# Two feed-forward stages of a decoder kernel, from loops over chunks to code written out as pipelines

## The reference

```python
def _layernorm(x, axis=-1, eps=1e-05):
    m = jnp.mean(x, axis=axis, keepdims=True)
    v = jnp.var(x, axis=axis, keepdims=True)
    return (x - m) / jnp.sqrt(v + eps)

def _L2_ffn_ref(x, weight, gate_w, lora_U, lora_V):
    scaling = 1.0 / lora_U.shape[1]
    B, S, D_in = x.shape
    xt = x.reshape(-1, D_in)
    gate = jax.nn.softmax(xt @ gate_w.T, axis=-1)
    base = xt @ weight.T
    t = jnp.einsum('nh,erh->ner', xt, lora_U)
    lora = jnp.einsum('ne,eor,ner->no', gate, lora_V, t)
    out = base + scaling * lora
    return out.reshape(B, S, -1)

def _L3_ffn_ref(x, weight):
    b_weight = jnp.sign(weight)
    return jnp.einsum('bsi,oi->bso', x, b_weight)
...
    x = x + _L2_ffn_ref(_layernorm(x, axis=-1), L2_ffn_weight, L2_ffn_gate_w, L2_ffn_lora_U, L2_ffn_lora_V)
...
    x = x + _L3_ffn_ref(_layernorm(x, axis=-1), L3_ffn_weight)
```

## Time and profile before

| | us |
|---|---|
| three runs | 3691.47, 3686.51, 3674.39 |
| median | 3686.51 |
| profiled execution, its time | 3691.43 |
| its span in the profile | 3689.4 |
| TensorE busy | 3116.8 (84%) |
| VectorE busy | 1856.5 (50%) |
| ScalarE busy | 1345.1 (36%) |

### The profile page before, as it was taken

The page is one execution under the profiler, slowest core; times in us unless marked ns, Lnnn a source line. Parts: engine busy times, 40 slices in busy tenths (PEclk is TensorE's granted clock), DMA queues, the critical chain, the costliest instruction groups (busy, mean ns, idle before and its releaser), DMA issues. The chain is left out here.

```text
span 3689.4 us, 47172 instructions
## 1 busy us (share of the span) xinstructions
PE 3116.8 (84%) x17330; PEld 1949.8 (53%) x17330; DVE 1856.5 (50%) x3060; ACT 1345.1 (36%) x2260; POOL 1142.4 (31%) x964
## 2 busy tenths in 40 slices
PE   5769999999999979999986929996867666898786
PEld 3444555545545458788844626764645543343354
DVE  3365666555666653242287521112568456556574
ACT  2223444444444443333243523332324233334452
POOL 0015666665666620000053331112323021011230
PEclk9879999999999989999988959997988776669987
DMA  3010000000000011111000071222010000000000
GB/s 109 0 48 1 1 1 1 1 1 1 1 1 1 1 36 52 52 41 52 14 14 32 1 258 27 34 33 47 2 31 1 6 9 2 1 1 1 10 18 26
DMA packets 110937, 89.27 MB, mean 24 GB/s; under 512 B 20459, under 2 KB 104197, under 8 KB 110725
## 3 DMA queue, kind: packets, MB, share of 16 engines
q1 hardware_dynamic: 101509, 75.73, 6.9%
q0 software_dynamic: 7152, 8.55, 1.3%
q10 hardware_dynamic: 2064, 2.10, 0.2%
HBM read 68.33 MB, written 18.94 MB: 24 GB/s over the span
## 5 line engine op out<-in xcount | busy, mean ns | idle before, releaser
L684 POOL TENSOR_TENSOR acc<-acc,pf 128x512 f32<-128x512 f32 (+1 forms) x448 | 564.1, 1281 | 254.2 <-ACT pf L811 254.0
L868 DVE TENSOR_REDUCE mxa<-ps 128x1 f32<-128x512 f32 x512 | 327.3, 681 | 229.1 <-PE ps L730 227.2
L811 ACT ACTIVATE pf<-ps 128x512 f32<-128x512 f32 x512 | 278.0, 595 | 318.7 <-PE ps L705 293.9
L718 PE MATMUL ps<-pf,v 128*64 128x512 f32 (+1 forms) x1152 | 311.0, 618 | 0.0
L3374 DVE TENSOR_REDUCE mx<-ps 128x2 f32<-128x1024 f32 (+1 forms) x192 | 184.0, 958 | 159.4 <-PE ps L3268 118.4
L3362 ACT ACTIVATE pT<-ps 128x1024 f32<-128x1024 f32 (+1 forms) x192 | 153.2, 811 | 222.3 <-PE ps L3280 221.8
L1678 POOL TENSOR_TENSOR e<-e,sm 128x1232 f32<-128x1232 f32 x48 | 107.9, 2249 | 228.7 <-DVE sm L1933 228.7
L730 PE MATMUL ps<-kH,qH 64*128 64x512 f32 x512 | 158.0, 443 | 23.9 <-DVE mc L876 18.5
L1065 POOL TENSOR_TENSOR x<-x,ys 128x256 f32<-128x256 f32 x16 | 11.9, 742 | 508.3 <-DVE ys L1270 508.3
L3264 PE MATMUL ps<-kT,qT 64*128 64x512 f32 (+2 forms) x384 | 102.1, 529 | 65.5 <-DVE mx L3374 58.9
L1736 PE MATMUL ps<-ident,e 128*77 128x128 f32 x768 | 123.9, 313 | 25.8 <-ACT pT L1843 24.6
(11 more groups left out here) (521 smaller groups left out, 7134.9 us busy)
## 6 DMA issues: line engine op xcount, KB each, us to landing
w_raw<-in_c_h SPq DMA_DIRECT2D x32, 512.0 KB, 3.9
w1a<-in_f_w SPq DMA_DIRECT2D x8, 1024.0 KB
w2a<-in_f_w SPq DMA_DIRECT2D x8, 1024.0 KB
moe_rows<-pad SPq DMA_DIRECT2D x1, 5167.5 KB, 20.1
xs<-moe_rows SPq DMA_DIRECT2D x39, 132.5 KB, 2.1
w_raw<-in_c_w SPq DMA_DIRECT2D x32, 128.0 KB, 2.3
x<-in_x SPq DMA_DIRECT2D x1, 2048.0 KB, 8.2
moe_acc<-x ACTq DMA_DIRECT2D x1, 2048.0 KB
```

The costliest lines, as they stand in the source:

```text
L684: pool.tensor_tensor(now[0:r, :], now[0:r, :], pf[0:r, n % RING, a, :], ALU.add).then_inc(added.sem, 1)
L718: ins = pe.matmul(g.bk(3)[SIDE[a], :], v[0:r, u // 2 % 2, t, u % 2 * P + a * HD:u % 2 * P + (a + 1) * HD], pf[0:r, n % RING, a, :], start= ...
L811: act.activation(pf[0:r, n % RING, a, :], g.bk(bk.bank[f"s{n}_{a}"])[0:r, :], ACT.Exp, bias=bias)\
L868: dve.tensor_reduce(mxa[:, q % 2, half, a, j:j + 1], g.bk(4 + a), AXX, ALU.max).then_inc(bk.release(f"m{q}_{i}_{a}"), 1)
```

## The change

In both stages `ln_block` is gone: its statistics are at the head of the one block that is left, before the chunks. The loops are written out, and the work of neighbouring chunks is interleaved. z and t have two buffers, zT three in the gated ffn and two in the last; ScalarE makes both copies of zT. In the gated ffn gates and parts of four tiles share two banks instead of four, tT has one, and the outputs rotate over three banks; in the last ffn the outputs rotate over six. The gate weights have a semaphore of their own. The output is stored two tiles at a time, 256 KB, as soon as they are added.

```diff
@@ -2762,96 +2762,162 @@
...
+        z, zT = sb("z", [P, 2, TC, D]), sb("zT", [P, 3, KD, CH])
+        t, gate, mx = sb("t", [P, 2, TC, E * R]), sb("gate", [P, TC, E]), sb("mx", [P, TC])
-        bk = Banks(g, [("t0", 0), ("t1", 1), ("p0", 2), ("p1", 3), ("p2", 4), ("p3", 5), ("tT", 6)]
-                   + [(f"y{j}", [7, 0, 1, 2][j]) for j in range(TC)])
...
-        ln_block(g, load_weights)
+        fills = []
+        for c in range(NC):
+            fills += [(f"t0_{c}", 0), (f"t1_{c}", 1), (f"p0_{c}", 2), (f"p1_{c}", 3), (f"tT_{c}", 4)]
+        fills += [(f"y{i}", 5 + i % 3) for i in range(NT)]
+        bk = Banks(g, fills)
...
+        parts = g.ps[:, 2:4, :].rearrange("p b (a n) -> p b a n", a=2)
...
+            @block.sync
+            def _(sp):
+                load(sp, gus[:], rows(gu), gate_in)
+                load(sp, w[:], rows(W), w_in)
+                load(sp, v[:], V, w_in)
...
-                with pe.Fori(0, NC) as c:
-                    pe.wait_ge(*z_made.at(c, 1))
-                    turn(g, pe, bk, c, ("t0", "t1"), z4)
...
+                def turn_tokens(c):
+                    pe.wait_ge(*z_made.at(0, c + 1))
+                    for k in range(KD):
+                        pe.wait_ge(*bk.free(f"t{k}_{c}", 0))
+                        for j in range(TC):
+                            ins = pe.transpose(g.bk(k)[:, j * P:(j + 1) * P], z[:, c % 2, j, k * P:(k + 1) * P], g.ident[:])
+                        ins.then_inc(bk.fill(f"t{k}_{c}"), 1)
+                def gates_and_parts(c):
+                    for k in range(KD):
+                        pe.wait_ge(*bk.read(f"t{k}_{c}", 0))
...
+                            for k in range(KD):
+                                ins = pe.matmul(g.bk(2 + b)[:, a * D:a * D + ER], zT[:, c % 3, k, j * P:(j + 1) * P], gus[:, k, :],
+                                                start=k == 0, stop=k == KD - 1)
+                        ins.then_inc(bk.fill(f"p{b}_{c}"), 1)
+                def output(c):
+                    pe.wait_ge(*t_made.at(0, c + 1))
+                    pe.wait_ge(*bk.free(f"tT_{c}", 0))
...
+                    for j in range(TC):
...
+                        pe.wait_ge(*bk.free(name, 0))
...
+                            pe.matmul(out, zT[:, c % 3, k, tile], w[:, k, :], start=k == 0, stop=False)
+                        pe.wait_ge(*bk.read(f"tT_{c}", 0))
+                        pe.matmul(out, tT[:, tile], v[:], start=False, stop=True).then_inc(bk.fill(name), 1)
+                turn_tokens(0)
+                pe.wait_ge(*gate_in.at(0, 16))
+                for c in range(-1, NC):
+                    if c + 1 < NC:
+                        gates_and_parts(c + 1)
+                    if c + 2 < NC:
+                        turn_tokens(c + 2)
+                    if c == 0:
+                        pe.wait_ge(*w_in.at(0, 32))
+                    if 0 <= c:
+                        output(c)
             @block.scalar
             def _(act):
-                with act.Fori(0, NC) as c:
-                    act.wait_ge(*bk.full("t0", c))
-                    act.activation(zT[:, 0, :], g.bk(0), ACT.Copy).then_inc(bk.release("t0"), 1)
...
+                def tokens(c):
+                    for k in range(KD):
+                        act.wait_ge(*bk.full(f"t{k}_{c}", 0))
+                        if c >= 3:
+                            act.wait_ge(*bk.full(f"y{TC * (c - 2) - 1}", 0))
+                        act.activation(zT[:, c % 3, k, :], g.bk(k), ACT.Copy).then_inc(bk.release(f"t{k}_{c}"), 1)
+                ln_stats_scalar(g, act, NT, spread, rooted)
+                tokens(0)
+                for c in range(-1, NC):
+                    if c + 2 < NC:
+                        tokens(c + 2)
+                    if c + 1 < NC:
+                        act.wait_ge(*logit.at(0, c + 2))
+                        act.activation(gate[:], gate[:], ACT.Exp).then_inc(expd.sem, 1)
+                    if 0 <= c:
+                        act.wait_ge(*bk.full(f"tT_{c}", 0))
+                        if c:
+                            act.wait_ge(*bk.full(f"y{TC * c - 1}", 0))
+                        act.activation(tT[:], g.bk(4), ACT.Copy).then_inc(bk.release(f"tT_{c}"), 1)
             @block.vector
             def _(dve):
-                with dve.Fori(0, NC) as c:
-                    link = Chain(dve, step, c)
-                    normalise(g, dve, c, z4).then_inc(z_made.sem, 1)
-                    dve.wait_ge(*bk.full("t1", c))
-                    dve.tensor_scalar(zT[:, 1, :], g.bk(1), 1.0, None, ALU.mult).then_inc(bk.release("t1"), 1)
...
+                link = Chain(dve, step, 0)
+                def normalised(c):
+                    if c >= 2:
+                        dve.wait_ge(*bk.full(f"t{KD - 1}_{c - 2}", 0))
...
+                        i = TC * c + j
+                        ins = dve.tensor_scalar(z[:, c % 2, j, :], g.x[:, i, :], g.mean[:, i:i + 1], g.rstd[:, i:i + 1], ALU.subtract, ALU.mult)
+                    ins.then_inc(z_made.sem, 1)
+                def gated(c):
+                    quad = lambda a: a.rearrange("p (b a) -> p b a", a=2)
+                    eight = mx[:].unsqueeze(2).broadcast_to([P, TC, E])
+                    for b in range(2):
+                        dve.wait_ge(*bk.full(f"p{b}_{c}", 0))
...
+                    link(dve.tensor_tensor(gate[:], gate[:], eight, ALU.mult))
+                    if c >= 2:
+                        dve.wait_ge(*bk.full(f"tT_{c - 2}", 0))
...
+                        ins.then_inc(bk.release(f"p{b}_{c}"), 1)
+                    for b in range(2):
+                        dve.wait_ge(*bk.read(f"p{b}_{c}", 0))
                     dve.sem_inc(t_made.sem, 1)
+                def added(c):
+                    for i in range(TC * c, TC * (c + 1)):
+                        dve.wait_ge(*bk.full(f"y{i}", 0))
+                        dve.tensor_tensor(g.x[:, i, :], g.x[:, i, :], g.bk(bk.bank[f"y{i}"])[:, 0:D], ALU.add).then_inc(bk.release(f"y{i}"), 1)
+                ln_stats_vector(g, dve, g.x, NT, spread, rooted, link)
+                normalised(0)
+                normalised(1)
+                for c in range(-1, NC):
+                    if c + 1 < NC:
+                        gated(c + 1)
+                    if c + 3 < NC:
+                        normalised(c + 3)
+                    if 0 <= c:
+                        added(c)
+                link.close()
...
@@ -2859,60 +2925,83 @@
...
+        w, z, zT = sb("w", [P, KD, D]), sb("z", [P, 2, TC, D]), sb("zT", [P, 2, KD, CH])
+        bk = Banks(g, [(f"t{k}_{c}", k) for c in range(NC) for k in range(KD)] + [(f"y{i}", KD + i % 6) for i in range(NT)])
+        STORE = 2
...
-        ln_block(g, load_weights)
             @block.sync
             def _(sp):
-                with sp.Fori(0, NC) as c:
-                    sp.wait_ge(*bk.read(f"y{TC - 1}", c))
-                    t = ds(c * TC, TC)
-                    sp.dma_start(out_t[:, t, :], g.x[:, t, :]).then_inc(stored.sem, 16)
-                sp.wait_ge(*stored.at(NC - 1, 16))
+                load(sp, w[:], rows(W), w_in)
+                for i in range(0, NT, STORE):
+                    for n in range(i, i + STORE):
+                        sp.wait_ge(*bk.read(f"y{n}", 0))
+                    sp.dma_start(out_t[:, i:i + STORE, :], g.x[:, i:i + STORE, :]).then_inc(stored.sem, 16)
+                sp.wait_ge(*stored.at(0, 16 * (NT // STORE)))
...
+                turn_tokens(0)
-                with pe.Fori(0, NC) as c:
...
+                for c in range(NC):
+                    if c + 1 < NC:
+                        turn_tokens(c + 1)
+                    for k in range(KD):
+                        pe.wait_ge(*bk.read(f"t{k}_{c}", 0))
...
             def _(act):
                 act.wait_ge(*w_in.at(0, 16))
                 act.activation(w[:], w[:], ACT.Sign).then_inc(signed.sem, 1)
-                with act.Fori(0, NC) as c:
-                    act.wait_ge(*bk.full("t0", c))
-                    act.activation(zT[:, 0, :], g.bk(0), ACT.Copy).then_inc(bk.release("t0"), 1)
+                ln_stats_scalar(g, act, NT, spread, rooted)
+                for c in range(NC):
+                    for k in range(KD):
+                        act.wait_ge(*bk.full(f"t{k}_{c}", 0))
+                        if c >= 2:
+                            act.wait_ge(*bk.full(f"y{TC * (c - 1) - 1}", 0))
+                        act.activation(zT[:, c % 2, k, :], g.bk(k), ACT.Copy).then_inc(bk.release(f"t{k}_{c}"), 1)
...
-                with dve.Fori(0, NC) as c:
-                    normalise(g, dve, c, z4).then_inc(z_made.sem, 1)
-                    dve.wait_ge(*bk.full("t1", c))
-                    dve.tensor_scalar(zT[:, 1, :], g.bk(1), 1.0, None, ALU.mult).then_inc(bk.release("t1"), 1)
...
+                link = Chain(dve, step, 0)
...
+                ln_stats_vector(g, dve, g.x, NT, spread, rooted, link)
+                normalised(0)
```

(65 more changed lines are left out.)

82 lines of the change are left out of this document (29 added, 53 removed).

## The result

| | us |
|---|---|
| before, median of four runs | 3680.45 (3674.14 to 3691.47) |
| changed, median of four runs | 3622.82 (3621.43 to 3630.18) |
| ratio, 95% interval | 0.9844 (0.9813 to 0.9876) |
| changed, profiled execution, its span | 3623.91, 3622.1 |
| forecast | 3646 (3634 to 3662) |

The account below looks back on a forecast made before the run. Bound: a serial chain in which TensorE and VectorE wait for each other. Gains of 27.4 (gated ffn), 12.0 (last ffn) and 0.8 (stores) make 40.2 us; 3691.4 - 40.2 - 4.9 gives 3646, range 3634 to 3662.

Parts of the forecast that it names:

- some 5: Whole kernel: how many us a median could be off, as the three runs of before spread over 17 us.
- The start: Gated ffn from its reciprocal: copies until 10.5 us, table load until 11.8, rest of gates and t until 13.9.
- Normalising chunk 2 is queued behind: 15.4: Gated ffn: VectorE normalises chunk 2 until 15.4 us, TensorE turns it until 17.0, then writes chunk 0's output.
- This first one I take at 8.5 because the clock has to rise in it: Gated ffn, chunk 0's output: 8.5 us where one at 2.4 GHz is 6.2, ending at 25.5.
- both holes: Last ffn: TensorE waits 2.1 us before the turn of chunk 2, with a second hole before chunk 3's.
- I take 5.0 for the first: Last ffn, first chunk's outputs: 5.0 us, between 6.62 in the first chunk and 3.72 in the last of before.
- The clock staying low: Rival, both stages: half low gives a gain near 20 us, nearly all low 0 to 10; about 3680; chance 0.08.
- Less overlap: Rival, both stages: an in-order engine stands where forecast free; gain 20 to 28 us, about 3663; chance 0.07.
- More than forecast: Rival, both stages: clock up from the first output on; gain 47 to 49 us, about 3638; chance 0.05.
- Slower by fetching straight code: Rival: engines must fetch the written-out loops, 58 us over 384 matmul rows, 0.15 each; over 3705 us; chance 0.02.
- The table load: Gated ffn, ScalarE, right before the first Exp: 1.28 us without drain; by the skill's 2.66 the stage is 1.4 longer.
- its own last sign: Whole kernel: the prediction is wrong if another stage moved by more than a few us.

Follow-up runs that it names:

- in order: Changed kernel, both stages still straight code in one block with new buffers and stores, but each chunk taken from begin to end, not interleaved: 3664.16 us.
- Exp first: Changed kernel with the gated ffn's first Exp ahead of the two copies of chunk 1 on ScalarE: 3627.95 us in one run.
- fill 70 with both edits: Changed kernel with 70 unread transposes ahead of each stage's first turn, first Exp ahead of chunk 1's copies, all last-ffn chunks normalised first: 3613.10 us, ratio 0.9843.

## Why the prediction missed its range

**What failed.** The order of the work and the gain by interleaving were right. What put the time outside the range is the base of the sum: the forecast took the median of three runs as good to "some 5", and it stood 12.3 us above the median of the 19 later runs of before. In the stages one step of the working failed, the gates of chunk 1, which it has nowhere, and the clock's terms were too cautious.

**The gated ffn, 2.2 us better than forecast, by two errors that nearly cancel, which is luck.** The start was right to half a microsecond: copies until 10.1 us from the reciprocal (10.5 forecast), the load until 11.4 (11.8), t at 13.4 (13.9). The step that failed follows: "Normalising chunk 2 is queued behind: 15.4. TensorE turns chunk 2, until 17.0, and then writes chunk 0's output". The working has no gates of chunk 1, neither here nor in front of the Exp, where TensorE stood free in it from 9.8 on. With two banks for gates and parts they could not run there: they need chunk 0's t done. They ran from 13.1 to 17.1 at 1.2 GHz, the turn until 18.8. The other error is "This first one I take at 8.5 because the clock has to rise in it": it rose in front of the output, in the 6 us of unbroken work behind the wait, and the output took 6.0 us, until the next gates. Together 24.7 where 25.5 was forecast. From there on 22.7 us for the forecast's 24.1: the periods took 8.65, 7.8 and 6.3 where 9.3, 8.2 and 6.6 stood.

**The last ffn, 4.0 us better, by terms mis-sized nearly all for one reason, the clock.** The order of work, both holes and their place were right. "I take 5.0 for the first", "outputs 4.0" and "1.5" for the turns are the terms: 3.6, 3.6 and 1.1 were measured, and 1.8 for the hole in place of 2.1. In the changed order the turns of chunks 0 and 1 stand unbroken ahead of the first outputs, 3.7 us of TensorE's work at the low level, and that is where the clock rose. I had priced with the first chunk of before, where only 2.0 us of turning and a gap of 0.9 stand there. The term of the first outputs is not firm: in two later runs it was 4.68, in one 3.85.

**The rivals.** The clock staying low did not happen. By the Trainium skill, TensorE: Matmul & The Clock Gate, A second HAM failure mode: psum-queue depth-cycling, this order, which goes round all eight banks, was to be feared; it did not come here, with a granted clock of 1.00 from 2927.2 to 2955.2 us. The page tells of a kernel whose TensorE idled often between its groups; here it idled 0.5 us in 28.05, so this trace shows that going round the banks alone does not bring the swing, and no more. "Less overlap" did not happen: the waits for the copy of tT are 1.4 us in all. "More than forecast", at a chance of 0.05, had nearly the right size (47 to 49 us for 46.5) and the right mechanism but for the wait before the gates of chunk 1: the clock was up from the first output on. Slower by fetching straight code: nothing of it in the stages, since in order they took 78.7 and 43.7 us where the loops took 84.2 and 51.7. That rival's price was also misread: the two stages have 208 + 96 = 304 rows of matmuls and not 384, so 58 us would be 0.19 for each.

**The table load.** It took 1.28 us, with 0.02 us between it and the Exp, behind copies that ended 0.02 us before. The 2.66 of the Trainium skill, ScalarE: Activation LUTs, What ACT_TABLE_LOAD costs, does not show: the trace decides for 1.28.

**The time.** Of the 23.2 us between forecast and median, 6.3 are terms of the two stages and the end. The other 17 are not in the stages at all. The sum went from 3691.4 down to the median of three runs, 3686.5, and took that as good to "some 5"; 19 runs of before gave 3674.2, 12.3 lower, with a range from 3666.8 to 3703.2. The rest, under 5, is no more than the runs scatter; what it is was not shown. The working held the untouched stages at "nothing", which holds in the mean to within the 3.6 us above and is wrong for one execution: the 411.4 us of the profile's own block were the longest seen (390.0 to 404.1 in the thirteen other profiles). By its own last sign, another stage moved by more than a few us, the prediction had counted itself wrong; the second profile of before shows that this sign cannot tell a wrong mechanism from the block's own scatter. With 3674.2 in place of 3686.5 the same gain of 40.2 gives 3634, and the measured 46.5 gives 3628.

## What to carry over

Where two engines wait for each other in turn, interleave neighbouring chunks, and price a TensorE wait that remains by its length and also by what runs behind it at half the clock (here as much again, for a wait of 3.76 us). Before a wait is priced, ask of every bank who gives it back and behind what: here two banks in place of four put the gates of chunk 1 behind a table load. And a gain of some tens of us in a program of thousands needs the base of more than three runs, or a sum over the changed stages alone.

## What I had not expected of the hardware

- The same program scatters by 17 us in one block (411.4 and 394.1), where the clock differs: 0.61 or 0.99 in the same 50 us.
- TensorE ran at 2.4 GHz behind waits of 1.2 us (Exp first), 1.5 us (fill 70 with both edits) and 1.8 us (last ffn), and at 1.2 GHz behind the wait of 3.75 us, in all seven traces that have it. In order, where 1.81 and 0.78 us of waiting stand close together with one turn between them, it stayed up in two chunks of the last ffn (3.69) and fell in the third (5.38). The loop of before, with waits of 2.07 to 2.10 and 0.86 us there, was down for most of two chunks and up in the last, in both of its traces.
- Transposes that nobody reads, ending 0.5 us before the real work, kept the clock up into it (gates 2.09 us for 3.97); ending 3.8 us before it they were worth next to nothing (0.2 us in the gated ffn).
